# Four of five norms scaled by VectorE from mean and power, in a one-core language model tower whose instruction orders are written out

## The reference

```python
h = ln(word_emb[x] + pos_emb[itok] + type_emb[mask]) * gamma + beta   # norm E
h = h + relu(linear_attention(ln(h)))            # norm P; 16 heads, 44 random features each
h = h + top2_of_32_prototype_ffn(ln(h))          # norm F; the two nearest prototypes, rank 16
h = h + causal_attention_with_rope(ln(h))        # norm R; 16 heads of 16
h = h + ternary_ffn(ln(h))                       # norm M; 256 -> 1024 -> 256
def ln(x): m = mean(x, -1); return (x - m) / sqrt(var(x, -1) + eps)
```

## Time and profile before

| what | us |
|---|---|
| median of 3 runs | 462.4 (460.88 to 462.6) |
| the profiled execution, whole | 467.38 |
| its span, first to last instruction | 465.6 |
| mean granted TensorE clock | 0.956 of full |

### The profile page before, as it was taken

One profiled execution on the slowest core, in us unless ns is written; L12 is line 12 of the kernel. 1 busy time (PEld: TensorE's weight loads), 2 busy tenths in 40 slices (PEclk: granted clock), 3 DMA queues, 4 the chain that ended last, 5 costly groups with the idle time before them and its releaser, 6 DMA issues.

```text
span 465.6 us, 13969 instructions
## 1 busy us (share of the span) xinstructions
PE 395.4 (85%) x5011; PEld 273.8 (59%) x5011; DVE 349.0 (75%) x937; ACT 275.8 (59%) x605; POOL 293.7 (63%) x431
## 2 busy tenths in 40 slices
PE   8966687699779889897879897999889999798786
PEld 3443445356556656675567666677667677576564
DVE  6356969888878877878796988788886797674552
ACT  1134865648486757584758685748583848364531
POOL 7667979986576667787867785645672544352120
PEclk9999769979998989999999999899997999998999
DMA  4686733554483947677787566666494655301001
GB/s 137 175 270 163 181 72 57 69 83 92 85 156 63 129 83 105 136 118 139 115 111 111 117 128 95 109 132 125 86 117 94 101 131 104 72 3 46 14 13 35
DMA packets 145844, 48.56 MB, mean 104 GB/s; under 512 B 137264, under 2 KB 143216, under 8 KB 145776
## 3 DMA queue, kind: packets, MB, share of 16 engines
q1 hardware_dynamic: 144144, 43.21, 49.9%
q0 software_dynamic: 1632, 4.46, 3.7%
HBM read 11.80 MB, written 2.36 MB: 30 GB/s over the span
## 4 chain that ended last, share of the span: by engine, by line
PE 33%; POOL 18%; DMA 14%; issue 14%; DVE 9%; ACT 6%; SPq 3%; another core or an unknown queue 1%; POOLq 0%; ACTq 0%; DVEq 0%
PE PS L1438 9%; DMA hgT<-hgs 4%; PE PS L2033 4%; PE PS L1778 3%; DMA qkT<-qs 3%; DMA rT<-split 2%; POOL split L693 2%; PE PS L2015 2%; PE PS L1506 2%; PE PS L1936 2%; DMA xTP<-xsP 2%; POOL wneg L608 2%; POOL stage_f L690 2%; POOL hgs L676 1%; PE PS L1898 1%
## 5 line engine op out<-in xcount | busy, mean ns | idle before, releaser
L1084 DVE TENSOR_REDUCE split<-PS 128x16 f16<-128x2048 f32 x16 | 36.8, 2298 | 6.9 <-PE PS L1506 6.5
L680 POOL TENSOR_TENSOR rstdR<-rstdR,consts 128x1 f32<-128x1 f32 x16 | 8.8, 553 | 37.9 <-DVE rstdR L1043 37.9
L690 POOL TENSOR_TENSOR stage_f<-stage_f 128x512 f32<-128x512 f32 x16 | 20.4, 1272 | 18.7 <-DVE stage_f L1072 8.8
L2015 PE MATMUL PS<-xTM,w1q 128*128 128x128 f16 x512 | 31.4, 219 | 0.0
L2015 PEld LDWEIGHTS PS<-xTM,w1q 128*128 128x128 f16 x512 | 28.6, 98 | 3.6 <-issue 3.6
L1778 PE MATMUL PS<-faT_hi,hgT 128*128 128x256 f16 x128 | 26.7, 295 | 4.0 <-DMA hgT<-hgs 4.0
L1172 ACT ACTIVATE xnR<-hres,nmeanR,rstdR 128x256 f32<-128x256 f32 x16 | 9.6, 599 | 32.1 <-POOL nmeanR L682 32.1
L1438 PE MATMUL PS<-wqkT_hi,xTP 128*128 128x512 f16 x64 | 22.6, 395 | 4.6 <-DMA xTP<-xsP 3.7
L658 POOL TENSOR_TENSOR qe<-qef,qe 128x704 f16<-128x704 f32 x16 | 24.3, 1521 | 1.8 <-issue 1.0
L1637 PEld LDWEIGHTS PS<-va,kp 128*88 128x88 f32 x256 | 21.8, 158 | 2.6 <-issue 0.7
L1461 PE MATMUL PS<-warm 128*128 128x512 f16 x94 | 22.0, 398 | 1.4 <-DVE warm L1139 1.4
(11 more groups left out here) (328 smaller groups left out, 1435.3 us busy)
## 6 DMA issues: line engine op xcount, KB each, us to landing
out<-outb SPq DMA_DIRECT2D x16, 128.0 KB
w<-in_w1T SPq DMA_DIRECT2D x1, 1024.0 KB
w<-in_w2T SPq DMA_DIRECT2D x1, 1024.0 KB
stage_p<-in_wqkT SPq DMA_DIRECT2D x1, 512.0 KB, 5.0
stage_f<-in_fbT SPq DMA_DIRECT2D x1, 512.0 KB
stage_f<-in_faT SPq DMA_DIRECT2D x1, 512.0 KB
stage_r<-in_rwqk SPq DMA_DIRECT2D x1, 512.0 KB
rT<-split SPq DMA_TRANSPOSE x26, 2.9
```

The lines of the kernel that those rows point to most:

```text
L690: g.tensor_tensor(rot[:, :, :].rearrange("p h d -> p (h d)"), rc[:, :], rs[:, :], ALU.add).then_inc(rot_ok, 1)
L1084: v.tensor_reduce(slots(SLOT - DH)[:, 0:H, DH - 1].rearrange("p (c j) -> p j c", j=4), PS[:, BANK["s1"]:BANK["s1"] + 4, :].rearrange("p j ...
L2015: last = pe.matmul(PS[:, BANK["m1"] + f // 4, f % 4 * P:(f % 4 + 1) * P], w1q[:, n % KC, f * P:(f + 1) * P], xT["M"][:, n, :], start=False ...
```

## The change

- For norms P, F, R and M, POOL's step `xrs` keeps the power and loses the negated mean. ACT's steps `Pxn`, `Fxn`, `Rxn` and `Mxn` (16 tiles each) are gone. In their place DVE has steps of the same names: one `tensor_scalar`, (h - mean) * rstd, 128x256 float32, SBUF to SBUF, with two per-partition scalars. It waits for the power and for the readers of the old `xn`; `Fxn` also for `xsq` on ACT. `Pag`, `Fag`, `Rag` and `Mag` wait for `xn_ok` instead of `nm_ok`.
- Norm E stays as it was: power and negated mean on POOL, ACT scales. Unused DVE branches (`Enm`, `Pnm`, ...) are removed.
- All five lists of `ORDER` are new. They hold the same steps, except that 64 norm steps move from ACT's list to DVE's. Which tiles go by PE or by DMA, and the PSUM banks, are unchanged.
- `WARM` is new: 30 dummy matmuls in front of steps instead of 53. `warm_up` has 97 instead of 94.

The diff, cut. The hunks of P equal those of R but for names and the wait on `lo_ok`, and so does M's; of the lists, the middle lines of POOL, DVE and PE are kept.

```diff
@@ -57,72 +57,72 @@
 ORDER = {
...
     "POOL": """
...
+        Frs Ers e2 rot dist rl Prs Mrs gsl esc hgl rol onl g eh Ers Rrs e2 Plo Mlo qel Frs Prs rot dist rl gsl Plo bb Mrs hgl esc rol eh onl Ers esc
+        e2 qel Prs Rrs Frs eh Mlo dist rot bb rl gsl hgl Ers onl rol esc Plo Mrs g Rrs Prs Frs Mlo qel Mrs dist rot e2 rl gsl hgl Plo eh onl rol bb
+        qel Rrs Ers Mlo Frs rot dist Mrs Prs rl gsl hgl bb Mlo rol esc onl eh Plo Rrs Frs bb qel Mrs Prs rot dist rl Mlo gsl hgl rol onl qel Rrs Plo
+        Frs bb Mrs rot dist rl gsl hgl rol qel Mlo Rrs bb Frs rot dist rl gsl hgl Mrs rol Mlo Rrs Frs Mrs dist rot rl gsl hgl Mlo bb Rrs rot rl bb Mrs
+        Mrs bb Mrs bb bb
...
     """,
     "DVE": """
...
+        gt ws hg od Pxn on zq3 rT2b rT1b diag qmx oV qb ngm qd hF Rst Rag hP Fst Rxn kmx Fag Est kmr RT Pst kb Fxn kd Eag rs2 rc FT rs1 Pag nd2 top
+        qlo tix zq4 gap ctl gt hg diag od Pxn on qmx rd qb ro qd ngm Est ws rV hF Rst hP Rag kmx Rxn hR Fst Fag kmr RT Eag kb Fxn kd Pst rc rs1 FT rs2
+        nd2 top qlo Mst Pag tix gap ctl gt ws hg Pxn od diag rd on ro qmx qb Est qd ngm Mag Eag hF rV Rst Rag hP kmx Rxn hR Fst Fag kmr RT Pst Mxn Fxn
+        kb kd rc rs2 FT rs1 Mst nd2 Pag top qlo tix Mag MV gap zrm gt Pxn hg ws rd diag ro ctl Est qmx ml2 qb ml1 od qd on ngm rV hF Rst Rag kmx hR hP
+        Rxn kmr Fst Pst Fag Pag RT Fxn kb Mxn Mst kd rs2 Eag Mag FT rc rs1 nd2 top Pxn tix qlo gap MV rd gt ws hg ctl ro diag qmx od qb on ml1 ml2 qd
+        ob ngm hF Rst Rag Est hP Rxn kmx hR RT Fst Fag kmr Pst Mxn Pag Fxn kb rs2 kd rs1 FT rc nd2 Mst top Eag tix Pxn qlo gap MV Mag rd gt ro hg Mxn
+        ctl ws diag ml1 ml2 od qmx on qb ngm qd ob hF Rst Rag Est hR Rxn hP kmx Fst Eag kmr RT Fag kb Mst Pst Fxn kd Pag FT rs2 rc nd2 rs1 Est top tix
+        qlo Eag Mag gap rd gt ws ro hg ctl Pxn Mxn diag ml1 od on qmx ml2 qb qd ob ngm hF Rst Rag Pst hP Rxn hR kmx RT Fst Pag kmr Fag Mst rc Fxn kb
+        rs2 kd rs1 FT Est nd2 Eag top qlo tix rd gap ro Pxn gt ws hg diag Mag ml1 ctl qmx qb ml2 qd od on ngm ob Pst kmx hF Pag Rst hP Est hR Rag Fst
...
     """,
...
     "PE": """
...
-        rqk kbc pvx Ftr Mtr qk prt pvT fh ctx m1 fQ v o m2 s1 rv y fK wo of kmxT Rtr s2 kbc rqk Ftr pvx qk prt Mtr pvT fh ctx m1 v o fQ s1 m2 y of rv
-        wo fK s2 Rtr kmxT kbc rqk pvx Ftr qk prt pvT fh ctx m1 fQ o v m2 s1 rv y of fK wo kmxT Rtr s2 kbc rqk Ftr qk prt pvx fh ctx m1 pvT v o fQ s1
-        m2 y rv of fK wo s2 kmxT Rtr kbc qk Ftr rqk prt pvx fh m1 ctx pvT v fQ o m2 s1 rv y of wo fK Rtr s2 kmxT kbc rqk Ftr pvx qk prt pvT ctx fh m1
-        fQ v o m2 s1 rv y fK wo of Rtr s2 kmxT rqk kbc qk Ftr m1 prt pvx fh ctx pvT v fQ o m2 s1 y rv of fK wo Rtr s2 kmxT rqk kbc pvx Ftr qk prt pvT
-        fh m1 ctx v fQ o s1 m2 y rv of fK wo s2 Rtr kmxT kbc rqk pvx Ftr qk prt fh pvT ctx m1 v fQ o m2 s1 rv y ont fK wo of kmxT Rtr s2 kbc rqk Ftr
...
+        kbc rqk Ftr pvx qk prt Mtr pvT fh ctx m1 fQ o v m2 s1 rv y fK of wo Rtr s2 kmxT rqk kbc Mtr Ftr qk prt pvx fh pvT ctx m1 o v fQ s1 m2 y rv wo
+        of fK s2 Rtr kmxT kbc rqk Ftr qk prt pvx fh pvT ctx m1 o v fQ m2 s1 y rv of wo fK Rtr s2 kmxT rqk kbc pvx Ftr qk prt pvT fh m1 ctx v fQ m2 o
+        s1 rv fK y of wo s2 kmxT kbc Rtr qk Ftr rqk prt pvx ctx fh pvT m1 o fQ v m2 s1 rv y of fK wo Rtr kmxT s2 kbc Ftr rqk prt qk pvx ctx fh pvT o
+        m1 fQ v m2 s1 rv y of wo fK Rtr s2 kmxT kbc rqk Ftr qk prt pvx ctx pvT fh m1 fQ o v m2 s1 rv y fK wo of kmxT Rtr s2 kbc rqk Ftr pvx qk prt pvT
+        fh ctx m1 o fQ v m2 s1 rv y of wo fK Rtr s2 kmxT rqk kbc pvx Ftr qk pvT prt m1 fh ctx m2 fQ v o s1 rv ont y fK wo of kmxT Rtr s2 kbc rqk Ftr
...
     """,
 }
@@ -135,17 +135,12 @@
 
 
 WARM = {
-    "qk": {0: 4},
-    "v": {0: 7},
-    "fQ": {0: 9},
-    "kmxT": {0: 4, 2: 2, 3: 4},
-    "ctx": {0: 5, 2: 1},
-    "ont": {0: 2},
-    "Ftr": {0: 2},
-    "prt": {0: 3},
-    "rT2p": {0: 2},
-    "y": {1: 3},
-    "Rtr": {15: 1},
+    "qk": {0: 3},
+    "fQ": {0: 5},
+    "kmxT": {0: 3},
+    "ctx": {0: 9},
+    "ont": {0: 3},
+    "Rtr": {0: 2, 15: 1},
     "Mtr": {14: 2},
     "m1": {15: 1},
     "m2": {15: 1},
@@ -678,9 +667,6 @@
                     wait(g, ag_ok["R"], 3 * t + 3)
                     wait(g, xn_ok["R"], t)
                     g.tensor_tensor(rstd["R"][:, 1:2], rstd["R"][:, 0:1], consts[:, :], ALU.pow).then_inc(rs_ok["R"], 1)
-                    g.wait_ge(rs_ok["R"], t + 1)
-                    g.tensor_scalar(nmean["R"][:, :], mv["R"][:, 0:1], rstd["R"][:, 1:2], -1.0, ALU.mult, ALU.mult)\
-                        .then_inc(nm_ok["R"], 1)
                 elif op == "rot":
                     wait(g, rope_ok, 3 * t + 3)
                     wait(g, rh1_ok, t)
@@ -969,15 +946,15 @@
                     v.bn_stats(stats["F"][:, :], h_of(t)).then_inc(ag_ok["F"], 1)
                 elif op == "Fag":
                     wait(v, ag_ok["F"], 3 * t + 1)
-                    wait(v, nm_ok["F"], t)
+                    wait(v, xn_ok["F"], t)
                     v.bn_aggr(mv["F"][:, :], stats["F"][:, :]).then_inc(ag_ok["F"], 1)
                     wait(v, ag_ok["F"], 3 * t + 2)
                     v.tensor_scalar(rstd["F"][:, 0:1], mv["F"][:, 1:2], RES_EPS, None, ALU.add).then_inc(ag_ok["F"], 1)
-                elif op == "Fnm":
+                elif op == "Fxn":
                     wait(v, rs_ok["F"], t + 1)
-                    wait(v, xn_ok["F"], t)
-                    v.tensor_scalar(nmean["F"][:, :], mv["F"][:, 0:1], rstd["F"][:, 1:2], -1.0, ALU.mult, ALU.mult)\
-                        .then_inc(nm_ok["F"], 1)
+                    wait(v, tr_ok["F"], t)
+                    wait(v, xsq_ok, t)
+                    v.tensor_scalar(xn["F"][:, :], h_of(t), mv["F"][:, 0:1], rstd["F"][:, 1:2], ALU.subtract, ALU.mult).then_inc(xn_ok["F"], 1)
                 elif op == "FT":
                     wait(v, hi_ok["F"], t + 1)
                     v.tensor_tensor(xT["F"][:, KC:, :].rearrange("p c n -> p (c n)"), PS[:, BANK["Ftr"], 0:D],
@@ -1037,15 +1014,14 @@
                     v.bn_stats(stats["R"][:, :], h_of(t)).then_inc(ag_ok["R"], 1)
                 elif op == "Rag":
                     wait(v, ag_ok["R"], 3 * t + 1)
-                    wait(v, nm_ok["R"], t)
+                    wait(v, xn_ok["R"], t)
                     v.bn_aggr(mv["R"][:, :], stats["R"][:, :]).then_inc(ag_ok["R"], 1)
                     wait(v, ag_ok["R"], 3 * t + 2)
                     v.tensor_scalar(rstd["R"][:, 0:1], mv["R"][:, 1:2], RES_EPS, None, ALU.add).then_inc(ag_ok["R"], 1)
-                elif op == "Rnm":
+                elif op == "Rxn":
                     wait(v, rs_ok["R"], t + 1)
-                    wait(v, xn_ok["R"], t)
-                    v.tensor_scalar(nmean["R"][:, :], mv["R"][:, 0:1], rstd["R"][:, 1:2], -1.0, ALU.mult, ALU.mult)\
-                        .then_inc(nm_ok["R"], 1)
+                    wait(v, tr_ok["R"], t)
+                    v.tensor_scalar(xn["R"][:, :], h_of(t), mv["R"][:, 0:1], rstd["R"][:, 1:2], ALU.subtract, ALU.mult).then_inc(xn_ok["R"], 1)
                 elif op == "RT":
                     wait(v, hi_ok["R"], t + 1)
                     v.tensor_tensor(xT["R"][:, KC:, :].rearrange("p c n -> p (c n)"), PS[:, BANK["Rtr"], 0:D],
@@ -1104,15 +1080,14 @@
                     v.bn_stats(stats["M"][:, :], h_of(t)).then_inc(ag_ok["M"], 1)
                 elif op == "Mag":
                     wait(v, ag_ok["M"], 3 * t + 1)
-                    wait(v, nm_ok["M"], t)
+                    wait(v, xn_ok["M"], t)
                     v.bn_aggr(mv["M"][:, :], stats["M"][:, :]).then_inc(ag_ok["M"], 1)
                     wait(v, ag_ok["M"], 3 * t + 2)
                     v.tensor_scalar(rstd["M"][:, 0:1], mv["M"][:, 1:2], RES_EPS, None, ALU.add).then_inc(ag_ok["M"], 1)
-                elif op == "Mnm":
+                elif op == "Mxn":
                     wait(v, rs_ok["M"], t + 1)
-                    wait(v, xn_ok["M"], t)
-                    v.tensor_scalar(nmean["M"][:, :], mv["M"][:, 0:1], rstd["M"][:, 1:2], -1.0, ALU.mult, ALU.mult)\
-                        .then_inc(nm_ok["M"], 1)
+                    wait(v, lo_ok["M"], t)
+                    v.tensor_scalar(xn["M"][:, :], h_of(t), mv["M"][:, 0:1], rstd["M"][:, 1:2], ALU.subtract, ALU.mult).then_inc(xn_ok["M"], 1)
                 elif op == "MV":
                     wait(v, hi_ok["M"], t + 1)
                     v.tensor_tensor(xT["M"][:, KC:, :].rearrange("p c n -> p (c n)"), PS[:, BANK["Mtr"], 0:D],
@@ -1294,11 +1265,6 @@
                     wait(a, lo_ok["o"], t + 1)
                     wait(a, of_ok, t)
                     copy(xT["o"][:, 0:KC, :].rearrange("p c n -> p (c n)"), PS[:, BANK["ont"], 0:D]).then_inc(hi_ok["o"], 1)
-                elif op == "Fxn":
-                    wait(a, nm_ok["F"], t + 1)
-                    wait(a, tr_ok["F"], t)
-                    wait(a, xsq_ok, t)
-                    normalise(xn["F"][:, :], h_of(t), "F")
                 elif op == "xsq":
```

(13 more changed lines are left out.)

118 lines of the change are left out of this document (34 added, 84 removed).

## The result

The changed kernel takes 475.72 us (median of 4 runs, 473.36 to 480.51), the kernel before on the same chip 462.5 (460.88 to 464.49): the ratio is 1.0232, 95% interval 1.0181 to 1.0283. By the ratio the change costs 10.7 us, by the medians 13.2, where a gain of 6 was forecast, and 475.72 is above the range's upper end of 470. The profiled execution took 473.36 us, its span 471.4, at a mean granted clock of 0.935 (before: 0.956).

What follows compares the result with a forecast made beforehand. No engine was taken as full; the chain ran through all, and work leaving POOL counted most. Terms -8.1 - 1.4 + 3.9 + 2.6 + 4.0 - 3 - 4 + 0 = -6.0 us gave 456.5 us, range 447 to 470.

Steps and rivals of the forecast that it cites:

- DVE against POOL: DVE norms stand behind POOL instructions on the shared port: 0.25 us per norm, +4.0 us; sum -10.0 without it.
- port rule: DVE in a 2-port mode and GpSimd exclude each other for a whole instruction, whichever started first going first.
- nine crossings: The nine ACT norms on the old chain, 5.0 us together, priced as DVE norms at 0.40 us each.
- the higher bound: POOL's next instruction always wins against the DVE norm: 0.6 us per norm, +9.4 us; the sum becomes -0.6.
- More work on DVE: 64 norms at 0.40 us add 25.6 us to DVE; 22 us off the chain at 0.12 per us: +2.6 us.
- the new warm-up list: Fewer dummy matmuls on PE, 4.6 us less work in the first 110 us, covered by idle time: 0.
- Orders: New engine lists: more room for DMAs, -3 us; POOL and ACT work removed off the chain lets lists gain, -4 us.
- Queueing on DVE: DVE steps between Rag and Rxn make the norm 0.43 us late on each crossing: +3.9 us.
- A: DVE becomes the bound in the middle, its chain share rising to perhaps a third: +8 us, 470; chance 0.26.
- B: The chain moves to PE, PSUM banks and rT's DMA, so about no change: -1.2 us, 461; chance 0.19.
- C: The lists pay in full for POOL's and ACT's relief: -16 us, 446; chance 0.12.
- D: The more room for DMA landings isn't there, so the -3 is 0: 459.5; chance inside the forecast's 0.43.

Runs made afterwards that it cites:

- 16: Changed kernel with each DVE norm replaced by a one-port reduction copying the first tile's normalised rows: 464.48 us, ratio 0.9908.
- 17: The changed kernel itself, run again on the chip of its one-port stand-ins: 474.64 us, ratio 1.0221.
- the repeats: Two further profiled executions of the unaltered changed kernel, in two later sets of runs: 475.23 us (ratio 1.0259) and 474.64 us (ratio 1.0221).
- experiment 3: Kernel before plus 64 spare one-port bn_stats on DVE beside its norms, result unused: 467.7 us, ratio 1.0149.
- experiment 10: Kernel before with only the changed kernel's WARM and warm_up: 464.94 us, ratio 1.0047.
- experiment 2: Kernel before, old lists and warm-up, with norms P, F, R and M moved to DVE without the negated mean: 475.83 us, ratio 1.0354.
- experiment 8: Changed kernel with each Rxn moved to right behind Rag in DVE's list: 480.83 us, ratio 1.0452.
- 12: The changed kernel itself, run again on another set's chip: 475.23 us, ratio 1.0259.

## Why the prediction was wrong

**The step that failed is "DVE against POOL", priced at +4.0 us.** It measured 10 to 14 us (16 against 17). Its size per norm was right: 0.40 alone and 0.25 of standing were put in, 0.41 and 0.255 came out (0.665 in all, 16.3 us over 64). The port rule of the Trainium skill's page "SBUF — State Buffer", section "SBUF: two separate sides", was the right one to weigh, and the trace agrees where POOL's instruction is a long one (a norm under `qel` ended 0.15 us after it), but not for POOL's powers: there the measurement decides, and they held no norm (last section).

What failed was the price of the standing: nine crossings at the mean of 0.25 us, 2.3 in full, and 0.12 per us for the rest. The norms on DVE are on the chain more often than ACT's nine were, and the ten longest of their 24 pieces stand 0.68 us each: 6.9 us of the 16.3 lie on the chain itself (4.1 and 6.4 in the repeats). With the other 9.4 us at the 0.26 of experiment 3 an estimate from these rows is 6.9 + 2.4 = 9.3 us, near the lower of the two measurements; the rest stays open.

The reason given against the higher bound, that the norm "comes 0.43 us late on average, so the collision is by chance", is half true. The norms of R began 0.27 us after their power, nine of the 16 within 0.1 us. Where the norm waited for the power alone, POOL's next step, if one was ready, began 0.03 to 0.07 us before the norm. Over all four norms 22 of 64 began within 0.1 us, with 8.8 of the 16.3 us; the 7.5 us of the other 42 are chance indeed. The stand per norm lay between the two ends that were priced, its effect on the time at or above the upper one (+9.4).

**More work on DVE, +2.6 us:** mis-sized too. A us of DVE work that nobody waits for costs 0.26 (experiment 3, 0.13 to 0.38), not the 0.12 that DVE's share of the old chain gave; for the 22 us off the crossings 5.7 instead of 2.6. Taking a share of the old chain as a marginal price assumes that the share stays, and it went from 9% to 21% (20% and 17% in the repeats).

**Without the collision the sum was -10.0 us; measured -4.3 (0.9908) and -2.1 (0.9955).** The dearer DVE work explains 3.1 of the 6 to 8 us missing, the new warm-up list, put at 0, perhaps another 2.2 (1.0047 in the old lists, experiment 10). With both the sum is -4.7, and with the collision at 10 to 14 it is +5 to +9, where +10.7 was measured. That is bookkeeping over single runs, not shown.

**Orders, -3 and -4 us:** the first was right in kind: the DMA share of the chain fell from 14% to 5%, hgT's wait from 3.2 to 0.5 us, more than the third foreseen, qkT's by 0.6 only. Both together, and the new `WARM` with them, measured -5.6 us (experiment 2 against the changed kernel), near the -7; but the two are of different sets of runs, and by their intervals it may be anything from 1 to 10.

**Queueing on DVE, +3.9 us:** from the end of variance plus eps to the end of norm R takes 1.65 us after, 1.68 before. So the negated mean saved and the queue and the stands together cost the same: nothing was won on R's path, where 0.31 us per norm is won without the stands (1.37 in 16). The norm was 0.23 us late (0.27 after the power, 0.04 at best), not 0.43. The queue as such was no loss that could be mended: without it the run took 6 us more by the medians and 9 by the ratios (experiment 8 against 12, two chips).

**The rivals.** A was the nearest (slower, 470), with its mechanism half right: PE's waits do name DVE steps, and POOL's next instruction is ready when the power ends, often `qel`, as its case said. But DVE didn't fill up: it has 35 us free in the middle where under 20 was the mark. A's share was counted as time on the chain per us of DVE work, 0.12 before; 21% of 471.4 us over 379.0 is 0.26 (0.25 and 0.21 in the repeats), at the 25% from which A was to decide. What A had too high was the norm, 1.13 us for 0.665. The larger part of the loss came from the stands, and plain DVE work was dearer as well. B and C are out; D is refuted by the DMA waits.

**The marks.** DVE busy 379.0 (375 to 390), POOL 279.5 (272 or more), ACT 242.8 (near 238), rT's wait (5.1) and single norms over 1 us under a POOL instruction came as written. The mean of the norms, 0.665, lay just over 0.65, and qkT's wait, which was to go, kept 1.7 us. PE's wait for norm R, 8.0 us against "shorter than 3.1", was the mark that showed the forecast wrong; since it is 5.9 in 16, most of that rise isn't the collision, and what it is stays open.

**Slips that change nothing:** the upper bound of the queue is 1.06 us per crossing by its own rows, not 1.03, and rival C's "nearly a tenth of each" is 8% of POOL's work but 14% of ACT's.
